# Two 16-head attention stages: the residual leaves PSUM on ScalarE with its bias, the gate is multiplied in by GpSimd once per chunk

## What is computed

```python
# second block, B, N = 64, 64; H, D = 16, 16
h = modulate(rmsnorm(x, norm1_w), sh_msa, sc_msa)
q, k, v = split(h @ qkv_w.T)
q, k = rmsnorm(q, q_norm_w), rmsnorm(k, k_norm_w)        # per head
q, k = rope3d(q), rope3d(k)
attn = softmax(einsum('bnhd,bmhd->bhnm', q, k) * scale)
o = einsum('bhnm,bmhd->bnhd', attn, v).reshape(B, N, C)
o = o @ proj_w.T + proj_b
x = x + g_msa * o                                        # this line is touched
# third block
h = _ln(x) * (1.0 + scale_msa) + shift_msa
...                                                      # q, k, v with biases, rope, softmax, y
attn_out = y @ out_w.T + out_b
x = x + gate_msa * attn_out                              # and this one
```

## Time and profile before

| | |
|---|---|
| median of 3 runs | 2206.26 us (2197.68 to 2216.82) |
| the profiled execution | 2202.69 us, its span 2200.9 us |
| PE busy | 1962.6 us (89%) |
| DVE busy | 1387.8 us (63%) |
| ACT busy | 1016.6 us (46%) |
| POOL busy | 825.0 us (37%) |
| stage A1 | about 897 to 1235 us of the span |
| stage A2 | about 1480 to 1771 us of the span |

### The profile page before, as it was taken

The page is one execution under the profiler, slowest core; times in us unless marked ns, Lnnn a source line. Parts: engine busy times, 40 slices in busy tenths (PEclk is TensorE's granted clock), DMA queues, the critical chain, the costliest instruction groups (busy, mean ns, idle before and its releaser), DMA issues. The chain is left out here.

```text
span 2200.9 us, 40916 instructions
## 1 busy us (share of the span) xinstructions
PE 1962.6 (89%) x15270; PEld 1524.0 (69%) x15270; DVE 1387.8 (63%) x2122; ACT 1016.6 (46%) x1725; POOL 825.0 (37%) x737
## 2 busy tenths in 40 slices
PE   5999999999997998588887799988999889998897
PEld 3788787888875776466666677766776667776674
DVE  3565665666564555488888567758888745553554
ACT  2444343444445665355655433324554556652322
POOL 2211211111013344567767433446677824340000
PEclk7999999999998999799998999999999999999998
DMA  5100000000010000100000000010000000003222
GB/s 176 68 1 2 2 1 2 1 1 1 1 39 25 0 0 1 43 1 2 0 1 1 26 0 0 0 39 2 2 0 1 2 29 0 0 1 104 87 68 77
DMA packets 25860, 44.57 MB, mean 20 GB/s; under 512 B 3952, under 2 KB 11952, under 8 KB 25584
## 3 DMA queue, kind: packets, MB, share of 16 engines
q1 hardware_dynamic: 25712, 42.48, 5.8%
HBM read 36.18 MB, written 6.29 MB: 19 GB/s over the span
## 5 line engine op out<-in xcount | busy, mean ns | idle before, releaser
L1169 DVE TENSOR_TENSOR Glb<-Gfb,Ghb 128x512 fp32r<-128x512 f32 x176 | 164.4, 943 | 101.1 <-ACT Ghb L1120 99.4
L321 POOL TENSOR_TENSOR Tm<-Dv,MOD 128x512 f32<-128x512 f32 x96 | 110.6, 1172 | 252.1 <-DVE Dv L378 163.4
L439 PE MATMUL bank<-HH,W1b 128*128 128x512 f32 x448 | 185.6, 414 | 13.4 <-PEq L1449 7.1
L439 PE MATMUL O<-Ghb,W2b 128*128 128x512 f32 x352 | 143.7, 408 | 47.4 <-DVE Glb L1169 45.7
L441 PE MATMUL bank<-HH,W1b 128*128 128x512 f32 x448 | 178.7, 399 | 0.0
L440 PE MATMUL bank<-HL,W1b 128*128 128x512 f32 x448 | 178.6, 399 | 0.0
L459 POOL TENSOR_TENSOR spare<-RT 128x1 f32<-128x1 f32 x32 | 6.5, 203 | 432.7 <-DVE RT L450 432.7
L310 POOL TENSOR_TENSOR XS<-Tm 128x512 f32<-128x512 f32 x48 | 69.9, 1456 | 220.5 <-ACT Tm L276 220.5
L441 PE MATMUL O<-Ghb,W2b 128*128 128x512 f32 x352 | 138.6, 394 | 0.0
L440 PE MATMUL O<-Glb,W2b 128*128 128x512 f32 x352 | 138.1, 392 | 0.0
L1600 ACT ACTIVATE PTa<-bank 128x512 f32<-128x512 f32 x128 | 69.8, 594 | 123.9 <-PE bank L1480 123.8
(11 more groups left out here) (258 smaller groups left out, 5362.4 us busy)
## 6 DMA issues: line engine op xcount, KB each, us to landing
w<-l_w_dram SPq DMA_DIRECT2D x33, 256.0 KB, 3.5
wm<-w_mods_dram SPq DMA_DIRECT2D x6, 768.0 KB, 5.7
X<-xT_dram SPq DMA_DIRECT2D x16, 256.0 KB, 6.7
out_dram<-XO SPq DMA_DIRECT2D x8, 512.0 KB, 2.7
W2b_f<-l_w_dram SPq DMA_DIRECT2D x11, 256.0 KB, 5.2
WQK_f<-l_wqk_dram SPq DMA_DIRECT2D x8, 256.0 KB, 8.8
W1b_0f<-l_w_dram SPq DMA_DIRECT2D x8, 256.0 KB, 3.5
WV<-l_wv_dram SPq DMA_DIRECT2D x1, 1024.0 KB, 10.2
```

The costliest lines, as they stand in the source:

```text
L321: nc.gpsimd.tensor_tensor(Tm[:, k].rearrange("p (b t) -> p b t", t=T), Dv[:, k].rearrange("p (b t) -> p b t", t=T), m, ALU.mult).then_inc( ...
L439: nc.tensor.matmul(out, w_lo_ap, x_hi, start=first, stop=False)
L1169: nc.vector.tensor_tensor(Gl[m % gb][:], gf, Gh[m % gb][:].bitcast(F32), ALU.subtract).then_inc(g_lo.h, 1)
```

## The change

The bias is added by ACT, which moves each half of the projection from `PJ` to `RTs[p]` with one ACTIVATE (Identity with a bias column). It stands at the start of ACT's step. DVE does nothing for the residual any more. The gate is multiplied by POOL inside `add`: two multiplications of 128x512 in place, a wait for both (`rt_g`), and then the addition as before.

```diff
+        rt_g = count("rt_g")
...
+                        def residual(tt, t, c, p):
+
+                            act.wait_ge(out_ready.h, out_ready.at(tt + 1))
+                            if t == 0:
+                                act.wait_ge(x_added.h, x_added.at(c - 1))
+                            for m in range(DH):
+                                col = BC[f"b_out{l}"] + m
+                                nc.scalar.activation(RTs[p][:, m, t * P:(t + 1) * P], PJ[:, m], ACT.Identity,
+                                                     bias=bias_cols[:, col:col + 1]).then_inc(out_taken.h, 1)
...
                         def step(c, t, p, more, tail=False, first=False):
                             tt = c * TL + t
                             prev = (t - 1) % TL
+                            if past(tt, 3):
+                                back = int(t < 3)
+                                residual(tt - 3, (t - 3) % TL, c - back, (p - back) % 2)
                             if ahead(t, more, tail, 2):
                                 act_square(act, tt + 2)
...
+                        residual(NT - 2, TL - 2, NCH - 1, 1)
                         oh(NT - 1, 1)
+                        residual(NT - 1, TL - 1, NCH - 1, 1)
...
-                        def residual(tt, t, c, p):
-
-                            dve.wait_ge(out_ready.h, out_ready.at(tt + 1))
-                            if t == 0:
-                                dve.wait_ge(x_added.h, x_added.at(c - 1))
-                            n = P // T
-                            for m in range(DH):
-                                nc.vector.scalar_tensor_tensor(
-                                    out=RTs[p][:, m, t * P:(t + 1) * P].rearrange("p (b k) -> p b k", k=T), in0=PJ[:, m].rearrange("p (b k) -> p b k", k=T),
-                                    scalar=bias_cols[:, BC[f"b_out{l}"] + m:BC[f"b_out{l}"] + m + 1],
-                                    in1=MOD[l][:, G_A, m, bass.ds(tt * n, n)].unsqueeze(2).to_broadcast([P, n, T]),
-                                    op0=ALU.add, op1=ALU.mult).then_inc(out_taken.h, 1)
-
                         def step(c, t, p, more, tail=False, first=False):
                             tt = c * TL + t
-                            if past(tt, 3):
-                                back = int(t < 3)
-                                residual(tt - 3, (t - 3) % TL, c - back, (p - back) % 2)
...
-                        for tt in (NT - 2, NT - 1):
-                            residual(tt, tt % TL, NCH - 1, 1)
...
                             pool.wait_ge(out_taken.h, out_taken.at(2 * TL * (c + 1)))
+                            for m in range(DH):
+                                g = MOD[l][:, G_A, m, bass.ds(c * CB, CB)].unsqueeze(2).to_broadcast([P, CB, T])
+                                rt = RTs[p][:, m].rearrange("p (b k) -> p b k", k=T)
+                                nc.gpsimd.tensor_tensor(rt, rt, g, ALU.mult).then_inc(rt_g.h, 1)
+                            pool.wait_ge(rt_g.h, rt_g.at(2 * c + 2))
                             nc.gpsimd.tensor_tensor(X[:, :, tok(c)], X[:, :, tok(c)], RTs[p][:], ALU.add).then_inc(x_added.h, 1)
```

More of the change, by code:

```diff
@@ L1751, in attention12 @@
                         c.passed(NT)
-                out_ready.passed(NT); out_taken.passed(2 * NT); x_added.passed(NCH)
+                out_ready.passed(NT); out_taken.passed(2 * NT); x_added.passed(NCH); rt_g.passed(2 * NCH)
         class Hyper:
```

## The result

The changed kernel takes 2216.67 us (median of 20 runs, 2211.88 to 2227.36) where the kernel before takes 2207.53 (20 runs): a ratio of 1.0052, 95% interval 1.0039 to 1.0065. The ratio stands for 11.5 us more (8.6 to 14.3); the medians themselves lie 9.1 apart. I go by the ratios throughout. The kernel is slower by half a per cent, and inside the range. The change added about 33 us of work to ACT and 31 to POOL and took 30 from DVE, and what it gained and lost nearly cancels.

The account below looks back on a forecast made before the run. A chain through several engines was taken to set each pass. Gains and losses summed to +5.4 us on the profiled 2202.69, giving 2208.1; the same difference on the median gave 2211.7, forecast as 2211, range 2196 to 2228.

Parts of the forecast that it names:

- POOL as the bound that takes the stalls' place: POOL's longer row in both stages swallows what PE's shorter stalls give: 2200 to 2222 us, chance 0.70.
- no `add` ahead: First pass of each stage, without POOL's addition ahead of it: gains 1.0 us in A1 and 1.4 in A2.
- Prices of the instructions: ACT gains 0.5 to 0.6 us per tile, DVE loses 0.60 per tile, POOL gains 2.38 per chunk.
- The stalls: PE's waits for the residual at t = 1 shrink from 2.5 to about 1.0 us in A1, vanish in A2.
- A1's 0.3 us that can be kept: In A1 POOL's next rope leaves 0.3 us of a stall shortened by 1.5; taken as 0.25 in four passes.
- The clock's 2.0 us: In A1 PE's clock mostly holds with stalls of 1.0 us, which gives 2.0 us back in two long passes.
- The sign that I had set for this term: The clock's gain is wrong if A1 still has stretches at 0.50 of over 4 us past 1120.
- The last passes: POOL's longer row costs 1.5 us in A1's last pass, 2.1 and 2.4 in A2's last two.
- The ends: Two multiplications and their wait lie bare ahead of each stage's closing barrier: 2.4 us each, 4.8 in all.
- rival 3: In A1 small DVE operations wait out whole POOL instructions, 3.4 us in six passes, 20 us: 2231; chance 0.17.
- a sign of rival 3: DVE's L1385 to L1389 together above 2.2 us in the passes of A1.
- Rival 2: PE's stalls go in both stages and nothing takes their place: 2183 us, halfway 2192 to 2199; chance 0.10 for both.

Follow-up runs that it names:

- e1: Changed kernel without the gate's multiplications on POOL and their wait, so only the residual's move from DVE to ACT is left: 0.9949 of the kernel before.
- e3: Changed kernel with POOL's two multiplications moved from `add` to the step t = 2 ahead, except each stage's last pair: 1.0007 of the kernel before.
- e11: Changed kernel executed once more, unaltered, for a second trace: span 2210.0 us, where its first execution had 2222.9.
- e6: Changed kernel with the gate in ACT's scale, four 128x64 ACTIVATEs a tile, no POOL multiplications, last chunk's residual on DVE: 2196.55 us, 0.9957 of the kernel before.
- e8: Kernel before executed once more, unaltered, for a second trace: span 2206.0 us, where its first execution had 2200.9.
- e5: Changed kernel with each stage's last chunk (tiles 28 to 31) keeping DVE's residual and no POOL multiplication for it: 1.0024 of the kernel before.
- e2: Kernel before with POOL's two multiplications and their wait put into `add` as well, DVE's residual kept: 1.0069 of the kernel before.
- e4: Changed kernel with POOL's two multiplications moved to t = 3, between rope and modulation, except each stage's last pair: 1.0046 of the kernel before.

## Where the prediction was right and where it failed

The forecast, POOL as the bound that takes the stalls' place, is what happened. e1 shows that the move gains and e3 that the place of POOL's multiplications decides whether the gain is kept; the six passes of the changed kernel together are as long as those before. The time is lost in the last pass and at the end of each stage. Means of both executions of each kernel, set against the terms of the sum (each row is good to some 2 us):

| us | forecast | measured |
|---|---|---|
| start to S[5], A1 | none | -1.1 |
| start to S[5], A2 | none | +0.9 |
| A1, S[5] to S[9], no `add` ahead | -1.0 | -1.8 |
| A1, S[9] to S[29] (4 x 0.25, clock 2.0) | -3.0 | +2.4 |
| A1, last pass | +1.5 | +3.6 |
| A2, S[5] to S[9], no `add` ahead | -1.4 | -1.8 |
| A2, S[9] to S[25] | 0 | -1.3 |
| A2, S[25] to S[29] | +2.1 | +2.4 |
| A2, last pass | +2.4 | +3.0 |
| both ends | +4.8 | +6.0 |
| sum | +5.4 | +12.3 |

The 12.3 of four traces agrees with the 11.5 of the runs. Mechanism and side were right, the size of the sum was half. In A2 each term came out within what a trace can tell; in A1 the passes from S[9] on and the last one are 7.5 us above their terms, which is more than the whole gap of 6.9.

*Prices of the instructions: right.* ACT's pair takes 0.61 us (forecast 0.5 to 0.6), POOL's pair 2.04, the wait behind it 0.08 to 0.19 and not 0.32, so the row grew by 2.1 to 2.23 for 2.38. ACT is 33 us busier, POOL 31. DVE is only 29.5 less busy for 38: its small operations take 41.1 us in A1 for 35.2.

*The stalls: right.* 1.04 us in A1 (forecast 1.0), none in A2 (a single one of 0.7 in e11). 29 us of waits for the rope, 19 to 24 of them new (forecast 10 or more for the rope and FB together).

*A1's 0.3 us that can be kept, and which operation is late next: wrong.* I compared the release with the rope behind the addition. PE needs another one first, that of the step before, which ends at 1085.21 and stands *ahead* of the multiplications [PE and POOL of the pass above]. PE comes 2 us too early for it, so 1.58 us of shorter stall brings little with any row behind it: L1468 starts only 0.3 us sooner in the pass, in e1 as in the changed kernel, and e1 keeps 0.9 a pass, of which a part may come from a clock that falls less (24 us at the lower level in the six passes, 28 to 31 before).

*The clock's 2.0 us: wrong.* It asked that stalls of 1.0 leave the clock up. But the stall is not shorter as a whole, it is in two parts, 0.96 and 1.99, with 1.1 us of work between. In the pass above, after the change:

```profile
1082.00:1086.00 4.00, 1.74 (x11) 1.51 (x12) 3.97 (x5) 2.26 (x6) 3.92 (x4) 0.89 0.00 0
1086.00:1090.00 4.00, 4.00 (x56) 3.63 (x55) 3.81 (x6) 2.14 (x5) 3.81 (x4) 0.68 0.00 0
```

The same two stretches of the kernel before:

```profile
1082.00:1086.00 4.00, 1.63 (x8) 1.57 (x8) 3.74 (x6) 1.74 (x5) 3.92 (x4) 0.74 0.00 0
1086.00:1090.00 4.00, 4.00 (x60) 3.45 (x59) 3.81 (x7) 2.66 (x7) 2.41 (x3) 0.83 0.00 0
```

The clock (third column from the right) falls later and stays down as long. The sign that I had set for this term, a stretch at 0.50 of over 4 us past 1120, is there, with PE busy in it:

```profile
1123.00:1132.00 9.00, 8.52 (x66) 7.83 (x67) 5.94 (x9) 4.65 (x10) 8.59 (x9) 0.50 0.01 3
```

By the granted clock, the six passes of A1 hold 31 and 28 us at the lower level in the two executions before and 34 in both of the changed kernel. In e3 and e6 they hold 10 and 14, and those are kernels with shorter passes.

*The last passes: the mechanism right, mis-sized in A1.* 3.6 us for 1.5. PE's waits of the last pass after the change:

```profile
1203.29 1.09 PE L1481 MATMUL bank<-ident,SPa 128*128 128x128 f32 x8 [1.78 <-ACT RT L1588]
1206.50 1.12 PE L1468 MATMUL bank<-ident,QNa 128*128 128x128 f32 x4 [2.11 <-POOL QNa L1425]
1217.55 0.66 PE L1468 MATMUL bank<-ident,QNa 128*128 128x128 f32 x4 [2.84 <-POOL QNa L1425]
```

Before there were 2.75 for the residual and 1.05 for ACT at the third place. The 2.84 is the row that I had reckoned with; the 2.11 is the rope ahead of it, which takes the shortened stall back and more. Behind the second the clock is down too: L1495, L1516 and L1532 take 1.93, 2.08 and 1.99 us where they took 1.13, 1.16 and 1.09, and the first two, 1.7 us of the 3.6, lie in this pass. In A2 the wait for the rope in the last pass is 4.94 us (3.33 in e11) where I had 1.30 + 2.4 = 3.7; the 1.30 does not repeat either, it is 2.85 in e8. What follows runs at the lower clock:

```profile
1765.74 1.12 PE L1468 MATMUL bank<-ident,QNa 128*128 128x128 f32 x4 [4.94 <-POOL QNa L1425]
...
1769.07 2.08 PE L1516 MATMUL O<-OSa,WOa 128*128 128x128 f32 x8
1771.08 1.99 PE L1532 MATMUL S<-KBa,QTa 64*64 64x256 f32 x16
```

Before and in the pass ahead they take 1.16 and 1.09. POOL at that place shows that the next stage's weights (L205) stand in the row as well:

```profile
1754.77 2.04 POOL L1722 TENSOR_TENSOR RTa<-RTa,MOD 128x512 f32<-128x512 f32 x2
1756.89 2.37 POOL L1724 TENSOR_TENSOR X<-X,RTa 128x1024 f32<-128x1024 f32 x1
1759.22 2.49 POOL L205 TENSOR_TENSOR W2b<-W2b_f,W2b 128x512 fp32r<-128x512 f32 x2
...
1764.43 1.26 POOL L1425 TENSOR_TENSOR QNa<-RAa,RBa 128x512 f32<-128x512 f32 x1
```

*The ends: the barrier right, some 0.6 us each missed.* POOL at the end of A2 (answers the earlier trace rows):

```profile
1785.95 2.04 POOL L1722 TENSOR_TENSOR RTa<-RTa,MOD 128x512 f32<-128x512 f32 x2 [10.43 <-ACT RTa L1588]
1788.08 2.34 POOL L1724 TENSOR_TENSOR X<-X,RTa 128x1024 f32<-128x1024 f32 x1
```

PE's wait at the barrier is 5.71 us where it was 3.57: 2.1. The rest stands ahead of it, where the clock is down behind the waits above: the last scores (L1532) take 1.99 us for 1.09 in both stages. e5, which has no multiplication there, still takes 0.6 more than before.

*The lock (rival 3): it is there, and I gave it no term.* In the pass of A1 shown:

```profile
1084.63 0.64 DVE L1386 SCALAR_TENSOR_TENSOR SSa<-SSa 128x32 f32<-128x32 f32 x1
1085.30 0.97 DVE L1388 SCALAR_TENSOR_TENSOR SSa<-SSa 128x32 f32<-128x32 f32 x1
1086.30 0.97 DVE L1390 SCALAR_TENSOR_TENSOR SSa<-SSa 128x32 f32<-128x32 f32 x1
```

The three take 2.58 us for 1.43 before, past the 2.2 that I had set as a sign of rival 3: they end at 1085.27, 1086.27 and 1087.27, each within 0.1 of the end of the POOL instruction beside it (the rope 1085.21, the first multiplication about 1086.19, the second 1087.21). The Trainium skill ("SBUF — State Buffer", Who interferes with whom) has this as an exclusive lock over whole instructions; by that rule, the trace agrees, with those three ends. DVE starts them 0.8 us earlier in the pass and ends them 0.3 later, and POOL has its own row to finish before it can use the result, so in the four passes like this one the lock costs little on top of the row. In the pass from S[25] rival 3's case does come, in both traces; L1390 misses the gap and waits for the addition:

```profile
1164.85 2.39 DVE L1390 SCALAR_TENSOR_TENSOR SSa<-SSa 128x32 f32<-128x32 f32 x1
```

The rope behind it then waits 0.85 us for DVE. Over A1 the small operations take 6 us more than before; what that is of the 11.5 was not parted from POOL's row. The 20 us of rival 3 did not come in the changed kernel. e1, e2 and e4 show that the lock takes more where the operations meet otherwise. What would be left without the lock was not tried (the small operands in another memory, so that only one comes from SBUF).

*Rival 2* fell to e1: even with POOL's row as before, 27.7 us of stalls were worth 11. What of the other 16 is the late rope's and what the lock's is open.

## What to carry to other kernels

Before a stall is taken away, list what the stalled engine takes up next from *each* other engine, with the time at which it is ready; here the second item was 2 us late, and took back more than the stall had given. Work for an engine that is "37% busy" is priced by the slack of what stands behind it in its queue, in every pass, and for the last pass and the barrier apart. Where two engines were seen to wait for one another's whole instructions, work out again which ones will meet when either starts sooner: an operation of 0.19 us became one of 2.28 in e1. Idle time of GpSimd beside VectorE's norm, which reads two SBUF tiles, was not to be had (e4, 1.0046 against 1.0007). A gate and a bias that are constant over a stretch of the free axis cost ScalarE nothing but shorter instructions when they come in as its scale and bias columns (1.26 us a tile for four of 128x64, against 0.61 for two of 128x128 and, once per four tiles, 2.04 on GpSimd).

## What was not expected of the hardware

Two stalls of 0.96 and 1.99 us with 1.1 us of matmuls between them took the clock to 1.2 GHz for as long as one stall of 2.5 us had (L1337's sixteen matmuls took 1.91 us behind them). Two ACTIVATEs out of PSUM of 128x128 with a bias take 0.354 us each and 0.61 together; one of 128x256 took 0.38, so half the columns, with a bias, took hardly less. And the lock works in both directions: in e4 POOL's pair of multiplications took 2.49 us instead of 2.04 beside DVE's norm, and in e1 a DVE operation of 128x32 took 2.28 us instead of 0.19 beside POOL's addition.
